# A four-layer graph network on one core: the edge list is written first, and layer 0's scaled rows get four buffers

## The chip, the cores and the metric

The kernel runs on one core of a Trainium2 chip. The core has TensorE (matrix products), VectorE, ScalarE and GpSimd (elementwise work), and SyncE (SP), which issues most DMAs; all run their own instruction streams and meet only at semaphores. The metric is the time of one execution in microseconds (us), lower is better.

## The reference

Four layers work on x, 3125 nodes by 256 features, over one list of 53125 edges (source, destination, weight), sorted by destination. Each adds its result to x and normalises the rows.

```python
x = _layernorm(x + _L0_gnn_ref(x, edge_index, L0_gnn_W, L0_gnn_b), axis=-1)
x = _layernorm(x + _L1_gnn_ref(x, edge_index, edge_weight, L1_gnn_W_rel, L1_gnn_b_rel, L1_gnn_W_root), axis=-1)
x = _layernorm(x + _L2_gnn_ref(x, L2_gnn_W, L2_gnn_att, src, dst), axis=-1)
x = _layernorm(x + _L3_gnn_ref(x, edge_weight, L3_gnn_W, L3_gnn_b, src, dst), axis=-1)
...
# layer 0
h = x @ W
...
deg = jax.ops.segment_sum(ones, col, num_segments=n)
dinv = jnp.where(deg > 0, jax.lax.rsqrt(deg), 0.0)
norm = dinv[row] * dinv[col]
msg = h[row] * norm[:, None]
out = jax.ops.segment_sum(msg, col, num_segments=n)
return jax.nn.relu(out + b)
```

Layers 1 and 3 sum weighted neighbour rows in the same manner; layer 2 is graph attention with 4 heads. The change touches only the preparation and the first loop of layer 0.

## The kernel before

The nodes form NT = 25 tiles of 128 rows (P). Everything is written out by hand, engine by engine, and the order of the code is the order of the work; each engine waits for semaphores with `wait_ge`.

**Preparation.** SP loads the edges as 128 partitions of 416 edges, x, the weights and the biases. VectorE splits each edge into six bf16 fields (LO, CODE, three parts of the weight, panel number) in `tab`; the last field is line 671, after which the semaphore `s_tab` stands at 6. Then it counts degrees: in 26 blocks it writes one-hots of destination digits (lines 690, 691), and TensorE sums them (line 1072). Block b waits for the count of block b-2. After that come attention weights (lines 723 to 733), the span of the destination groups (lines 737 to 756), the degrees (761) and, with ScalarE (479), `dinv` (764).

**What SP sends behind the loads**, in this order: `dst_i`, the destination numbers reordered for layer 2, in pieces of 20 bytes (KC = 5 numbers; lines 317, 319); `src_all`, the source numbers reordered in the same way from DRAM to DRAM (lines 320, 322, 323; the last takes zeros from `spare`); after a wait for `s_tab`, the edge list `flat` (lines 326, 327); after a wait for its landing (`s_flat`), `etab`, 3322 overlapping rows of 128 edges in DRAM (line 330). POOL waits for `etab`, clears an accumulator (441), gathers 32 rows of it (428) and marks which edges belong to the tile (432 to 437); TensorE takes these when it starts the next stage (line 1144). `src_all` is read in layer 1 only (line 357).

**The first loop of layer 0**, over the 25 tiles, makes y = (x W) dinv in three bf16 parts, `y0p[:, t, 0..2]`. TensorE transposes x (line 1119) and multiplies (line 1130). VectorE copies the transposed x out (770). ScalarE's `scaled(t)` writes the f32 row into `u2` (487) and the first part (488). VectorE subtracts, leaving the rest in `u2` (779); ScalarE rounds the rest to the second part (496); VectorE subtracts again for the third part (782, semaphore `b_p3`). `u2` has two buffers, so 487 of tile t waits for 782 of tile t-2. `y0p` lies over the edge table in `big1`, so ScalarE waits for `s_flat` ahead of the loop (line 490). When the last `b_p3` has come, TensorE starts the stage that builds and applies the adjacency matrix, tile by tile; layers 1 to 3 follow.

## Time and profile before

| | us |
|---|---|
| time, median of 3 runs (lowest to highest) | 1800.18 (1798.89 to 1801.12) |
| the profiled execution's own time | 1804.56 |
| its span, first to last instruction | 1802.8 |
| edge list issued by SP | 67.97 |
| first scaled row of the loop (L487) | 81.30 |
| end of the loop (last L782) | 128.70 |

TensorE is busy for 88% of the span, VectorE for 66%. The span is cut into stages with different limits, so these shares say little about one stage. To see what a stage costs, one reads the timeline (start, duration, engine, line, and in brackets the idle time before and what ended it) and looks at which wait ends last. In the span of 1802.8 us, the adjacency stage of layer 0 begins at 129.1 us.

### The profile page before, as it was taken

Reading aid. Unit: us, or ns where it says so; the run is one execution under the profiler, and the core shown is the slowest. Engines: PE = TensorE matmul, PEld = TensorE weight load, DVE = VectorE, ACT = ScalarE, POOL = GpSimd, SP = SyncE. Lnnn points to the kernel's source line nnn. Section 1 sums busy time; section 2 is a strip of 40 time slices with the busy share of each in tenths; the row PEclk is TensorE's granted clock in tenths of the full one; section 3 lists DMA queues with packets and bytes.
Section 4 is the critical chain, followed back from the end, with each engine's and each line's share of the span. In section 5 each row is a group of like instructions: output and inputs, shape, how many; then the busy total and the mean of one; then the engine's idle time right before and its main releaser. Section 6 shows DMA issues by size and latency. Waiting matters only on the chain.

```text
span 1802.8 us, 37754 instructions
## 1 busy us (share of the span) xinstructions
PE 1594.0 (88%) x13731; PEld 1299.1 (72%) x13731; DVE 1186.2 (66%) x2739; ACT 512.2 (28%) x996; POOL 513.5 (28%) x540
## 2 busy tenths in 40 slices
PE   4568999999999899999958888888988877999998
PEld 4448878888888588888835666656666655888887
DVE  8468999999999322222259999998999976112111
ACT  0152232323232000000045555555555544000000
POOL 0022212121211200000157777777777700000000
PEclk9898999999999999999959999998999979999999
DMA  7921212121212434444234444444444421444440
GB/s 136 59 75 77 114 78 113 78 113 78 113 78 112 187 119 159 158 140 144 79 88 112 112 113 113 112 113 112 113 113 113 107 112 37 157 158 161 170 176 17
DMA packets 81220, 203.71 MB, mean 113 GB/s; under 512 B 42635, under 2 KB 57327, under 8 KB 71439
## 3 DMA queue, kind: packets, MB, share of 16 engines
q1 hardware_dynamic: 60047, 141.94, 24.9%
q0 software_dynamic: 20992, 59.37, 12.7%
q8 instruction: 113, 1.85, 0.4%
q14 instruction: 68, 0.56, 0.1%
HBM read 153.00 MB, written 53.57 MB: 115 GB/s over the span
## 4 chain that ended last, share of the span: by engine, by line
PE 55%; POOL 15%; issue 11%; DVE 10%; SPq 4%; DMA 2%; ACT 2%; DVEq 1%; POOLq 0%; ACTq 0%
PE bank L1228 30%; POOL ring L466 15%; PE bank L1172 9%; PE bank L1164 5%; PE bank L1157 2%; PE bank L1190 2%; SPq L322 2%; DVE work L797 2%; PE bank L1314 2%; DMA ring<-attention_rows,work 1%; PE bank L1236 1%; DVE big L810 1%; PE bank L1181 1%; DVE stats L815 1%; DMA edge_list<-big 1%
## 5 line engine op out<-in xcount | busy, mean ns | idle before, releaser
L466 POOL DMA_INDIRECT ring<-attention_rows,work x420 | 399.0, 950 | 149.9 <-issue 146.3
L1228 PE MATMUL bank<-big,ring 128*128 128x256 f32 x1250 | 273.0, 379 | 0.9 <-DVE x_sb L835 0.9
L1228 PE MATMUL bank<-big 128*128 128x256 f32 x1250 | 272.9, 379 | 0.0
L1228 PEld LDWEIGHTS bank<-big,ring 128*128 128x128 f32 x1250 | 236.5, 190 | 33.4 <-DVE x_sb L835 1.7
L1228 PEld LDWEIGHTS bank<-big 128*128 128x128 f32 x1250 | 236.6, 190 | 31.7
L1314 PE MATMUL bank<-work,ring 128*65 128x48 f32 x3360 | 238.6, 232 | 9.7 <-ACT work L587 9.1
L1314 PEld LDWEIGHTS bank<-work,ring 128*65 128x65 f32 x3360 | 227.8, 147 | 18.3 <-ACT work L587 16.2
L1172 PE MATMUL bank<-big 128*128 128x256 bf16 x1875 | 209.0, 273 | 0.9
L1172 PEld LDWEIGHTS bank<-big 128*128 128x128 bf16 x1875 | 181.4, 98 | 25.3 <-ACT big L509 4.7
L587 ACT ACTIVATE work<-work 128x960 f32<-128x960 f32 x84 | 161.8, 1926 | 84.2 <-DVE work L984 83.2
L1053 DVE TENSOR_TENSOR u<-bank,bias 128x256 f32<-128x256 f32 x25 | 10.6, 424 | 211.5 <-PE bank L1228 211.5
L810 DVE SCALAR_TENSOR_TENSOR big<-big,ring,bank 128x400 f32<-128x400 f32 x200 | 125.1, 628 | 35.0 <-PE bank L1164 28.7
L797 DVE TENSOR_TENSOR work<-work,ring 128x1600 bf16<-128x1600 bf16 x156 | 147.4, 985 | 0.0
L1164 PE MATMUL bank<-work 128*128 128x100 bf16 x2400 | 144.9, 209 | 0.0
L514 ACT ACTIVATE std<-mv,epsc 128x1 f32<-128x1 f32 x100 | 29.4, 294 | 386.4 <-DVE mv L816 385.8
L1297 PE MATMUL bank<-ident 128*32 128x512 bf16 x420 | 129.6, 409 | 0.0
L1289 PEld LDWEIGHTS bank<-ident,work 96*128 96x128 f32 x336 | 45.5, 195 | 109.8 <-DVE work L965 107.7
L1164 PEld LDWEIGHTS bank<-work 128*128 128x128 bf16 x2400 | 122.8, 98 | 0.0
L1289 PE MATMUL bank<-ident,work 96*128 96x96 f32 x336 | 59.6, 302 | 67.2 <-DVE work L965 66.5
L428 POOL DMA_INDIRECT ring<-edge_rows,cur x26 | 24.7, 949 | 310.8 <-PE bank L1144 310.7
L509 ACT CAST big<-bank 128x400 bf16<-128x400 f32 x200 | 96.6, 496 | 52.1 <-PE bank L1157 50.6
L951 DVE TENSOR_TENSOR work<-work,bank 128x960 f32<-128x960 f32 x84 | 96.0, 1143 | 0.7 <-issue 0.4
(214 smaller groups left out, 1981.4 us busy)
## 6 DMA issues: line engine op xcount, KB each, us to landing
adjacency<-big SPq DMA_DIRECT2D x25, 1600.0 KB, 5.2
ring<-adjacency SPq DMA_DIRECT2D x25, 1600.0 KB, 7.0
big<-adjacency SPq DMA_DIRECT2D x25, 1600.0 KB, 7.2
ring<-attention_rows,work POOLq DMA_INDIRECT x420
edge_rows<-edge_list SPq DMA_DIRECT2D x1, 4983.0 KB
x_sb<-in_x SPq DMA_DIRECT2D x1, 3072.0 KB
out_x<-xnT SPq DMA_DIRECT2D x24, 128.0 KB, 4.4
work<-attention_rows SPq DMA_DIRECT2D x168, 1.1 KB
```

What stands on the lines that cost most here:

```text
L466: G.indirect_dma_start(out=rows[0:EP, s, c, 0:ZG], out_offset=None, in_=ztab[:, :], in_offset=bass.IndirectOffsetOnAxis(ap=idx[:, g, c:c + ...
L509: S.copy(ac[:, :, q * QUAD * PAN:(q + 1) * QUAD * PAN], cnt_banks[q % 2][:, 0:NT * QUAD * PAN].rearrange("p (b d) -> p b d", b=NT)).then_i ...
L587: S.activation(prob[:, k % 2, :, :], val[:, k % 3].rearrange("p a c -> p c a"), ACT.Exp).then_inc(y["prob_ready"], 1)
L797: ins = V.tensor_tensor(oh[h][2][:, j], oh[h][1], repeated(digs[h][:, W1 + j], NT * PAN), ALU.mult)
L810: V.scalar_tensor_tensor(out=part, in0=part, scalar=keep[:, bass.ds(r, 1)], in1=w_banks[q % 2][:, 0:NT * QUAD * PAN].rearrange("p (b d) -> ...
L951: V.tensor_tensor(val[:, k % 3].rearrange("p (h w) c -> p h w c", h=H), pen[:, k % 3].unsqueeze(1).to_broadcast([EP, H, WIN, KC]), lg.rear ...
L1164: ins = mm(w_banks[b][:, 0:NT * QUAD * PAN].rearrange("p (b d) -> p b d", b=NT)[:, :, cols], lo[:, g, :, m], wtd[:, j, g, :, m].rearrange( ...
L1172: ins = mm(out_banks[t % 2][:, 0:D], ac[:, b, :], y0p[:, b, j, :], start=False, stop=False, skip_group_check=True)
L1228: ins = mm(bank[:, 0:D], slots[s][:, b, :], ybuf[:, b, :], start=(b == 0), stop=(b == NT - 1))
L1289: ins = mm(mb_bank[:, j * 2 * WIN:(j + 1) * 2 * WIN], mg[:, j:j + 1].to_broadcast([2 * WIN, P]), ident[0:2 * WIN, 0:2 * WIN], start=True, ...
L1297: mm(bank[0:32, :].rearrange("p (a b) -> p a b", a=4), ident16[:, 0:32], columns, start=True, stop=True, skip_group_check=True)
L1314: ins = mm(sum_banks[k % 3][0:FH, h * WIN:(h + 1) * WIN], rows[0:EP, s, c, h * FH:(h + 1) * FH], prob[:, k % 2, c, h * WIN:(h + 1) * WIN], ...
```

## The change

The edge list is sent directly behind the bias loads. The destination reordering follows it, then the edge rows `etab`, then the source reordering. `spare` becomes a tile of its own, outside `big1`. The scaled rows go into `ys`, with DEPTH = 4 buffers, carved out of `work`. On VectorE the second subtraction of a tile is made two tiles later, ahead of the first subtraction of the tile in hand.

```diff
+DEPTH = 4
...
+        spare = sb("spare", [EP, KC], I32)
...
-        spare = carve(EP, KC, dt=I32)
...
+        carve = carver(work)
+        ys = carve(P, DEPTH, D)
...
+            sp.wait_ge(s_tab, 6)
+            sp.dma_start(flat[0:P * COLS, :].rearrange("(p e) f -> p e f", p=P), tab[:]).then_inc(s_flat, 16)
+            sp.dma_start(flat[P * COLS:P * COLS + GRAN, :].rearrange("(a e) f -> a e f", a=1),
+                         tab[P - 1:P, COLS - GRAN:COLS, :]).then_inc(s_flat, 16)
             sp.dma_start(dst_i[:, 0:FULL, :], dst[0:FULL * EP * KC].rearrange("(g p k) -> p g k", p=EP, k=KC)).then_inc(
                 ld_dsti, 16)
             sp.dma_start(dst_i[0:REST, FULL, :], dst[FULL * EP * KC:E].rearrange("(p k) -> p k", k=KC)).then_inc(ld_dsti, 16)
+            sp.wait_ge(s_flat, 32)
+            sp.dma_start(etab[:, :], bass.AP(flat.tensor, 0, [[GRAN * FIELDS, ROWS + 1], [1, P * FIELDS]])).then_inc(s_etab, 16)
             sp.dma_start(src_all[:, 0:FULL, :], src[0:FULL * EP * KC].rearrange("(g p k) -> p g k", p=EP, k=KC)).then_inc(
                 s_srcs, 16)
...
-            sp.wait_ge(s_tab, 6)
...
-            sp.wait_ge(s_flat, 32)
...
-                if t >= 2:
-                    act.wait_ge(b_p3, t - 1)
+                if t >= DEPTH:
+                    act.wait_ge(b_p3, t - DEPTH + 1)
                 h = out_banks[t % 2][:, 0:D]
-                S.activation(u2[:, t % 2, :], h, ACT.Copy, scale=dinv[:, t:t + 1]).then_inc(b_y, 1)
+                S.activation(ys[:, t % DEPTH, :], h, ACT.Copy, scale=dinv[:, t:t + 1]).then_inc(b_y, 1)
...
-                    S.copy(y0p[:, t - 1, 1, :], u2[:, (t - 1) % 2, :]).then_inc(b_p2, 1)
+                    S.copy(y0p[:, t - 1, 1, :], ys[:, (t - 1) % DEPTH, :]).then_inc(b_p2, 1)
...
-            for t in range(NT + 1):
+            for t in range(NT + 2):
                 if t + 1 < NT:
                     xT_copy(t + 1)
+                if t >= 2:
+                    v = ys[:, (t - 2) % DEPTH, :]
+                    dve.wait_ge(b_p2, t - 1)
+                    V.tensor_tensor(y0p[:, t - 2, 2, :], v, y0p[:, t - 2, 1, :], ALU.subtract).then_inc(b_p3, 1)
                 if t < NT:
+                    v = ys[:, t % DEPTH, :]
                     dve.wait_ge(b_y, t + 1)
                     dve.wait_ge(b_p1, t + 1)
-                    V.tensor_tensor(u2[:, t % 2, :], u2[:, t % 2, :], y0p[:, t, 0, :], ALU.subtract).then_inc(b_r1, 1)
-                if t >= 1:
-                    dve.wait_ge(b_p2, t)
-                    V.tensor_tensor(y0p[:, t - 1, 2, :], u2[:, (t - 1) % 2, :], y0p[:, t - 1, 1, :],
-                                    ALU.subtract).then_inc(b_p3, 1)
+                    V.tensor_tensor(v, v, y0p[:, t, 0, :], ALU.subtract).then_inc(b_r1, 1)
```

SP's order behind the bias loads, before (tile names without buffer numbers; `big` holds `dst_i` and `tab`, `source_nodes` is `src_all`, `edge_list` is `flat`, `edge_rows` is `etab`):

```order
L316 DMA bias<-in_L_gnn_b 128x256
L317 DMA big<-in_dst 128x83x5
L319 DMA big<-in_dst 1x5
L320 DMA source_nodes<-in_src 128x83x5
L322 DMA source_nodes<-in_src 5x1
L323 DMA source_nodes<-big 127x5
L326 DMA edge_list<-big 128x2496
L327 DMA edge_list<-big 1x96
L330 DMA edge_rows<-edge_list 3322x768
```

and in the changed kernel, whose lines are numbered a little higher:

```order
L320 DMA bias<-in_L_gnn_b 128x256
L322 DMA edge_list<-big 128x2496
L323 DMA edge_list<-big 1x96
L325 DMA big<-in_dst 128x83x5
L327 DMA big<-in_dst 1x5
L329 DMA edge_rows<-edge_list 3322x768
L330 DMA source_nodes<-in_src 128x83x5
L332 DMA source_nodes<-in_src 5x1
L333 DMA source_nodes<-spare 127x5
```

The edge list moved from behind both reorderings to ahead of them, and the edge rows to between them.

VectorE at the start of the loop before, with the buffer numbers (L770 copies transposed x, L779 is the first subtraction, L782 the second):

```order
L770 COPY xnT<-bank1 128x256
L779 TENSOR_TENSOR u<-u,big1 128x256
L782 TENSOR_TENSOR big1<-u,big1 128x256
L770 COPY xnT<-bank6 128x256
L779 TENSOR_TENSOR u<-u,big1 128x256
L782 TENSOR_TENSOR big1<-u,big1 128x256
```

and in the changed kernel (L773 the copy, L787 the first subtraction, L782 the second):

```order
L773 COPY xnT<-bank6 128x256
L782 TENSOR_TENSOR big1<-work,big1 128x256
L787 TENSOR_TENSOR work<-work,big1 128x256
L773 COPY xnT<-bank1 128x256
L782 TENSOR_TENSOR big1<-work,big1 128x256
L787 TENSOR_TENSOR work<-work,big1 128x256
```

The second subtraction stands ahead of the first now and belongs to the tile two before; the scaled rows lie in `work` in place of `u`.

## Rows read from the trace of the kernel before

**Rows 1.** Page, section 4: shares of the span by line, of the chain that ended last.

```profile
PE bank L1228 30%; POOL ring L466 15%; PE bank L1172 9%; PE bank L1164 5%; PE bank L1157 2%; PE bank L1190 2%; SPq L322 2%; DVE work L797 2%; PE bank L1314 2%; DMA ring<-attention_rows,work 1%; PE bank L1236 1%; DVE big L810 1%; PE bank L1181 1%; DVE stats L815 1%; DMA edge_list<-big 1%
```

**Rows 2.** Timeline, SP: start us, us, engine, line, operation, destination<-source, count.

```profile
22.52 0.43 SPq L317 DMA_DIRECT2D big<-in_dst  x1
...
31.21 2.59 SPq L320 DMA_DIRECT2D source_nodes<-in_src  x1
...
33.84 33.62 SPq L322 DMA_DIRECT2D source_nodes<-in_src  x1
...
67.97 1.23 SPq L326 DMA_DIRECT2D edge_list<-big  x1
...
81.30 0.80 SPq L330 DMA_DIRECT2D edge_rows<-edge_list  x1
```

**Rows 3.** Timeline: last field, dinv, first products, first scaled row [idle before <-releaser].

```profile
17.93 0.86 DVE L671 CAST big<-big 128x416 bf16<-128x416 f32 x1
...
69.29 0.32 DVE L764 RECIPROCAL dinv<-dinv 128x25 f32<-128x25 f32 x1 [0.29 <-ACT dinv L479]
...
70.05 2.08 PE L1130 MATMUL bank<-ring,xnT 128*128 128x256 f32 x4
...
72.35 1.92 PE L1130 MATMUL bank<-ring,xnT 128*128 128x256 f32 x4
...
81.30 0.47 ACT L487 ACTIVATE u<-bank,dinv 128x256 f32<-128x256 f32 x1 [12.04 <-DMA edge_list<-big]
```

**Rows 4.** Timeline, layer 0's loop, tile 6 (L487 to the next L487).

```profile
92.75 0.47 ACT L487 ACTIVATE u<-bank,dinv 128x256 f32<-128x256 f32 x1 [0.69 <-DVE big L782]
...
93.03 1.13 PE L1130 MATMUL bank<-ring,xnT 128*128 128x256 f32 x4 [0.47 <-DVE xnT L770]
...
93.12 0.47 ACT L488 ACTIVATE big<-bank,dinv 128x256 bf16<-128x256 f32 x1
...
93.48 0.40 ACT L496 CAST big<-u 128x256 bf16<-128x256 f32 x1
...
93.69 0.42 DVE L779 TENSOR_TENSOR u<-u,big 128x256 f32<-128x256 f32 x1 [0.72 <-ACT big L488]
...
94.04 0.42 DVE L782 TENSOR_TENSOR big<-u,big 128x256 bf16<-128x256 f32 x1
...
94.37 0.42 DVE L770 COPY xnT<-bank 128x256 f32<-128x256 f32 x1
...
94.57 0.47 ACT L487 ACTIVATE u<-bank,dinv 128x256 f32<-128x256 f32 x1 [0.69 <-DVE big L782]
```

**Rows 5.** Timeline row of TensorE's restart; windows: busy by engine, PEclk, DMA share, GB/s.

```profile
83.06 2.07 PE L1130 MATMUL bank<-ring,xnT 128*128 128x256 f32 x4 [8.41 <-DVE xnT L770]
...
72.00:76.00 4.00, 2.64 (x9) 1.82 (x7) 0.00 (x0) 0.00 (x0) 0.00 (x0) 1.00 0.91 53
...
84.00:88.00 4.00, 4.00 (x13) 3.09 (x12) 1.17 (x4) 1.83 (x5) 0.00 (x0) 0.50 0.73 276
...
88.00:92.00 4.00, 3.19 (x16) 2.36 (x15) 2.32 (x7) 2.63 (x8) 0.00 (x0) 0.99 0.73 276
```

**Rows 6.** Timeline: last scaled row, and TensorE's first operation of the next stage.

```profile
126.43 0.47 ACT L487 ACTIVATE u<-bank,dinv 128x256 f32<-128x256 f32 x1 [0.68 <-DVE big L782]
...
129.14 0.38 PE L1144 MATMUL bank<-ident,ring 32*128 32x32 bf16 x5 [3.12 <-DVE big L782]
```

**Rows 7.** Timeline and windows: VectorE idle in the counting; stretch 57 to 69 us.

```profile
44.10 0.69 DVE L690 TENSOR_TENSOR work<-ring,big 128x1024 bf16<-128x1024 bf16 x1 [1.78 <-PE bank L1072]
...
55.47 0.69 DVE L690 TENSOR_TENSOR work<-ring,big 128x1024 bf16<-128x1024 bf16 x1 [3.04 <-remote]
...
57.00:69.00 12.00, 4.36 (x28) 3.08 (x26) 9.60 (x32) 0.00 (x0) 0.00 (x0) 1.00 1.51 6
```

**Rows 8.** Timeline: VectorE's first read of dst_i, POOL's first work on etab.

```profile
61.88 0.37 DVE L737 CAST dstf<-big 128x415 f32<-128x415 int32 x1
...
103.77 2.77 POOL L441 MEMSET big<- 128x3200 f32 x1 [100.78 <-DMA edge_rows<-edge_list]
```

More of the change, by code:

```diff
@@ L323, in _ @@
             sp.dma_start(src_all[REST:EP, FULL, :], spare[REST:EP, :]).then_inc(s_srcs, 16)
-            sp.wait_ge(s_tab, 6)
-            sp.dma_start(flat[0:P * COLS, :].rearrange("(p e) f -> p e f", p=P), tab[:]).then_inc(s_flat, 16)
-            sp.dma_start(flat[P * COLS:P * COLS + GRAN, :].rearrange("(a e) f -> a e f", a=1),
-                         tab[P - 1:P, COLS - GRAN:COLS, :]).then_inc(s_flat, 16)
-            sp.wait_ge(s_flat, 32)
-            sp.dma_start(etab[:, :], bass.AP(flat.tensor, 0, [[GRAN * FIELDS, ROWS + 1], [1, P * FIELDS]])).then_inc(s_etab, 16)
             sp.wait_ge(s_nswb, 1)
@@ L629, in _ @@
             V.memset(src_e[96:P, :], 0)
-            V.memset(spare, 0)
+            V.memset(spare[:], 0)
             V.memset(w_e[96:P, :], 0.0).then_inc(s_pad, 1)
```

## The prediction

> **What bounds the kernel now.** I read the page first, then the chain of work that ended last, then the DMA queue's rows, then the timeline of 17 to 130 us. The chain's shares put TensorE and the attention gathers in front, and neither is touched. But the chain also holds 2% on the SP queue's line 322 and 1% on the landing of the edge list [rows 1]. Those are the stretch that the change is about, so only 17 to 129 us has to be worked out; behind it every stage waits for the one before and should just shift.
>
> The reader is to see three things there. First, SP. It issues the 20-byte reordering of the destinations at 22.52 and of the sources at 31.21, and then stands in the issue of the next small transfer, line 322, for 33.62 us, until 67.5. Only then can it issue the edge list (67.97), whose end it waits for before it issues the edge rows at 81.30 [rows 2]. The edge list's last field had been written on VectorE by 18.8 [rows 3]. Second, ScalarE. 1/sqrt(degree) is ready at 69.6 and the product of tile 0 ends at 72.13, yet the first scaled row is written at 81.30, after 12.04 us idle put down to the edge list's landing [rows 3]; it waits for that because y0p lies over the edge table. Third, the loop over 25 tiles that follows is bound by no engine. ScalarE writes the scaled row (L487), writes its bf16 part (L488), VectorE subtracts (L779) and then makes the third part of the tile before (L782), and L782 frees one of two buffers for the next L487. Starts: 92.75, 93.12, 93.69, 94.04, 94.57, that is 0.37 + 0.57 + 0.35 + 0.53 = 1.82 us a tile, while each engine is busy 1.1 to 1.4 of it [rows 4].
>
> **The change part by part.**
>
> *The edge list goes first.* In SP's order its two transfers now stand behind the bias loads, whose last issue ends at 22.5, right ahead of the destinations. The wait for the table (18.8) is over by then, so it adds nothing; queued behind it are the destinations, wanted by VectorE's L737, which starts at 61.88 without idle time [rows 8]. Two issues (1.23 and 0.28 us) push them back by 1.6 of some 30 us to spare. The transfer is 624 KB; alone in the queue I estimate under 6 us, worked out from the edge rows, 4983 KB in at most 22.5 us (81.30 to POOL's start at 103.77) [rows 2, 8]. So it lands before 35. ScalarE's wait then ends with the product of tile 0: 70.05 + 2.08 + about 0.04 = 72.17 in place of 81.30, which is **9.1 us**.
>
> *The wait for the list's landing on SP* now stands behind the destinations. Queued behind it are the edge rows and the three source transfers. SP comes to it after the small destination transfer, near 33, so the edge rows go out then, and land by 33 + 22.5 = 56, where they landed at 103.8. POOL's first memset, gather and three operations took 103.77 to about 111.6 and would be done by 66, then beside VectorE's serial chain; 0 to 0.5 us for that. TensorE wants their result at the end of the loop, so this path stays hidden with some 45 us to spare. The sources come last: issued near 34, moving behind the edge rows, some 57 to 97. Their user is the index load in layer 1, far behind; SP's first adjacency store wants the queue at about 133, and is free by 92.
>
> *spare* moves to a tile of its own: same memset, no cost.
>
> *Four buffers and the later subtraction.* No instruction is added. What binds next? In the new order the subtraction of tile t stands right ahead of the copy of x of tile t+2. So the ring goes copy to product, product to ScalarE, L487 to L779, L779 to copy, and closes after two tiles: 0.48 (94.37 less one period is 92.55, to 93.03) + 1.13 + 0.04 + 0.94 (92.75 to 93.69) + 0.35 = 2.94, **1.47 us a tile** [rows 4]. ScalarE's three alone need 3 x 0.37 = 1.10, VectorE's three 1.03, TensorE about 1.3 to 1.4. Below it the bound is TensorE's 1.3; above it the old 1.82. I take 1.47, as every link of it is a row. The buffers themselves are behind by then: L487 of tile t waits for the third part of tile t-4, which stands two tiles back on VectorE.
>
> *How the loop runs.* L487 of tile 0 at 72.17; tile 1 at 72.35 + 1.92 + 0.04 = 74.31 [rows 3]; the product of tile 2 can start at 74.5. Its pace is the question. In 83 to 88 four passes took 2.07 us at a granted clock of 0.50, the lower level (1.2 GHz), after idle time; from 88 on the row says 0.99, the upper level (2.4 GHz), and they take 1.13 [rows 4, 5]. At 70 to 74 they also take 2.08, though the row there says 1.00 [rows 5]: I go by the durations, as low. The restart at 83.06 took about 4.9 us of work; from the first transpose at 68.9 that gives 73.8. So tile 2 runs fast: L487 at 75.7. Each tile that stays slow costs 2.14 less 1.47, so 0 to 4 tiles more are 0 to 2.7 us; I take 0 and keep the end.
> The Trainium skill (TensorE: Matmul & The Clock Gate, "Seeing it yourself") warns that clock events in a trace have been unreliable. By that the column at 72 to 76 is wrong and the sum stands; by the column the slowness of the first two products would have another cause, and if that lasted over the loop, 22 tiles at 2.14 would add 15 us, which the fast tiles from 88 on speak against.
>
> Tile 24: 75.7 + 22 x 1.47 = 108.0. From L487 of tile 6 (92.75) to tile 24 (126.43) before, 18 periods took 33.68, 0.9 more than 18 x 1.82; I keep that 0.9. The tail, last L487 to the end of the last L782, is 128.70 - 126.43 = 2.27, and TensorE starts the next stage on it [rows 6]. End: 108.0 + 0.9 + 2.3 = 111.2 against 128.70, **17.5 us** in all: 9.1 from the wait, 8.4 from the loop.
>
> *What is not in the rows.* While the sources moved, VectorE stood idle four times in 42 to 56 us, 1.78, 0.47, 0.88 and 3.04 us (6.2 in all), with the counts that it waits for already made by the order of the work; the first and last stand in [rows 7]. None stands in its 18 blocks before, and none in 57 to 69, when the sources were still moving (DMA share 1.51, 6 GB/s) [rows 7]. If the reordering causes them, they leave this stretch, which is serial before the loop, -6.2 us. They may then come back in 72 to 97: 6.2 in the 27 us from 42 to 69 is 0.23 a us, times 25 us, +5.7. If it does not, 0. All three middles are near zero, so I take 0 and keep -6.2 and +5.7 for the range.
>
> **The rivals.**
> *The stalls leave and do not come back*: the loop asks for fewer instructions a us than the counting did, and 57 to 69 had none. 1782.7 - 6.2 = 1776.5.
> *The loop hardly quickens*: another ring, a slow clock or returning stalls keep it at 1.7 to 1.82. For it: three engines hand on to each other five times a tile, and each hand-over is only known from the old order. Against it: no link of the old ring is left. With 1.82, 22 x 0.35 = 7.7 comes back: 1790.4; with 1.65, 1786.7.
> *It does not do what it says*: the edge list lands no earlier than the degrees, or the edge rows (POOL) become the late ones. It would need them 45 us later than worked out. Within 3 us of 1800.
> *Slower*: one mechanism, the source reordering beside the loop. A stall of the mean kind seen (6.2/4 = 1.55 us) on VectorE has nothing to hide it, since the four buffers cover ScalarE and not VectorE's own queue. Place: L782 and L787 of the changed loop, 72 us to its end. It decides from 17.5/1.55 = 11.3, so 12 stalls in 25 tiles undo the gain, and one in every tile gives 25 x 1.55 = 38.8 less 17.5, +21: 1821. Against it: four stalls in 27 us of the same transfers, and none in the last 12.
>
> **How the numbers follow.** The profiled execution took 1804.56 us, its span 1802.8 and 1.8 around it; the median of the runs shown is 1800.18, 4.4 lower, and I take the same difference off both: 1787.1 for a profiled execution, 1800.18 - 17.5 = **1782.7** as the time. Chances: forecast within 3.5 us 0.46; stalls leave or a period nearer 1.3, 0.18; slow loop 0.27; no effect 0.05; slower 0.04. The range 1774 to 1792 takes the first three with their ends (1776.5 less up to 2.5 for a shorter period; 1790.4 and 1.6 for the clock), and leaves 0.14. Faster by over 0.2% (3.6 us, about what a measurement can tell from no change) 0.93, within it 0.03, slower 0.04.
>
> **What would show it.** SP: the edge list issued near 23, no wait of ScalarE for it, its first L490 near 72.2. Edge rows issued near 33 and POOL's first memset before 60. In the loop L490 to L490 alternating about 1.2 and 1.7, mean 1.47; TensorE's first turn of fields near 111.5. The adjacency, attention and last layers as long as before. Wrong would be: POOL later than TensorE at the loop's end, a mean period over 1.65, "remote" or unexplained idle time on VectorE between 72 and 97, or VectorE waiting for the destinations at L740.

## The result and the profile after

The changed kernel takes 1778.49 us (median of 4 runs, 1777.58 to 1779.33) against 1799.54 us of the kernel before (4 runs, 1797.31 to 1801.12): a ratio of 0.9885, 95% interval 0.9869 to 0.9901, that is 21.05 us less. 1782.7 with a range of 1774 to 1792 was forecast. The profiled execution took 1778.9 us, its span 1777.1; the profiled one before lies 5.0 above the median of its four runs, so the two traces differ by more than the times do, 25.7 us.

Of these 25.7 us, 25.15 lie ahead of the first operation of the adjacency stage, which TensorE starts at 103.99 instead of 129.14. The rows in the order of the steps, first SP's (timeline; columns as in [rows 2]):

```profile
20.47 0.43 SPq L322 DMA_DIRECT2D edge_list<-big  x1
20.95 0.29 SPq L323 DMA_DIRECT2D edge_list<-big  x1
21.28 0.38 SPq L325 DMA_DIRECT2D big<-in_dst  x1
21.70 8.56 SPq L327 DMA_DIRECT2D big<-in_dst  x1
30.31 2.46 SPq L329 DMA_DIRECT2D edge_rows<-edge_list  x1
32.81 13.18 SPq L330 DMA_DIRECT2D source_nodes<-in_src  x1
46.03 43.77 SPq L332 DMA_DIRECT2D source_nodes<-in_src  x1
```

The edge list leaves at 20.47 instead of 67.97 [rows 2], the edge rows at 30.31 instead of 81.30. The long issue has not gone: SP stands 43.77 us in L332, but nothing that is wanted soon is queued behind it. Its next job, the first adjacency store, is at 125.82.

The serial part and the first tile (timeline, the changed kernel; L767 is L764 of before, L1134 is L1130, L490 is L487, L782 and L787 are the second and the first subtraction, L1148 is L1144):

```profile
62.67 0.32 DVE L767 RECIPROCAL dinv<-dinv 128x25 f32<-128x25 f32 x1 [0.29 <-ACT dinv L482]
63.43 2.08 PE L1134 MATMUL bank<-ring,xnT 128*128 128x256 f32 x4
65.60 0.47 ACT L490 ACTIVATE work<-bank,dinv 128x256 f32<-128x256 f32 x1 [2.96 <-PE bank L1134]
65.72 1.19 PE L1134 MATMUL bank<-ring,xnT 128*128 128x256 f32 x4
...
103.99 0.38 PE L1148 MATMUL bank<-ident,ring 32*128 32x32 bf16 x5 [2.74 <-DVE big L782]
```

Against [rows 3] two things are seen. ScalarE's wait for the edge list (12.04 us) is now a wait for the product, 2.96 us. And `dinv` itself is there at 62.67 instead of 69.29, 6.6 us earlier, which the change does not touch directly. The loop (two tiles; compare [rows 4], where one took 1.82 us):

```profile
89.34 0.47 ACT L490 ACTIVATE work<-bank,dinv 128x256 f32<-128x256 f32 x1 [0.70 <-PE bank L1134]
...
90.28 0.43 DVE L787 TENSOR_TENSOR work<-work,big 128x256 f32<-128x256 f32 x1 [0.74 <-ACT big L491]
90.43 0.47 ACT L490 ACTIVATE work<-bank,dinv 128x256 f32<-128x256 f32 x1
90.62 0.42 DVE L773 COPY xnT<-bank 128x256 f32<-128x256 f32 x1
...
91.10 1.13 PE L1134 MATMUL bank<-ring,xnT 128*128 128x256 f32 x4 [0.49 <-DVE xnT L773]
...
92.27 0.47 ACT L490 ACTIVATE work<-bank,dinv 128x256 f32<-128x256 f32 x1 [0.71 <-PE bank L1134]
```

Two tiles take 2.93 us, 1.09 and 1.84 in turn. ScalarE's idle time now ends on the product and no longer on the second subtraction. From tile 2 (68.52) to tile 24 (101.28) the mean is 1.489.

POOL's path (timeline; compare 103.77 in [rows 8]):

```profile
72.45 2.77 POOL L444 MEMSET big<- 128x3200 f32 x1 [69.46 <-DMA edge_rows<-edge_list]
75.38 1.22 POOL L431 DMA_INDIRECT ring<-edge_rows,cur  x1 [0.17 <-issue]
94.50 0.32 POOL L435 TENSOR_SCALAR cur<-cur 32x1 int32<-32x1 int32 x1 [17.90 <-DMA ring<-edge_rows,cur]
94.91 1.06 POOL L437 TENSOR_SCALAR ring<-ring,panel 32x128 bf16<-32x128 int16 x1
96.05 0.61 POOL L440 TENSOR_TENSOR ring<-ring 32x128 bf16<-32x128 bf16 x1
```

It is done at 96.7, 7.3 us ahead of TensorE's first turn of the next stage; some 45 us were forecast.

The chain that ended last, by engine, in shares of the span, before and after:

```profile
PE 55%; POOL 15%; issue 11%; DVE 10%; SPq 4%; DMA 2%; ACT 2%; DVEq 1%; POOLq 0%; ACTq 0%
PE 57%; POOL 15%; DVE 13%; issue 12%; ACT 1%; DMA 1%; DVEq 1%; POOLq 0%; SPq 0%; ACTq 0%
```

SP's 4% are gone, and the DMA's 2% are 1%; that 1% is the attention rows' landing. The large lines of [rows 1] keep their shares.

### The profile page after: what moved, and what is told of

Same layout as the page of the kernel before. It is cut to its first block, busy times and chain, and to the rows that moved or that the text cites. A ratio compares the mean times of both kernels' runs of the same rounds, so it can differ in the third digit from the quotient of the medians.

```text
span 1777.1 us, 37754 instructions
## 1 busy us (share of the span) xinstructions
PE 1588.4 (89%) x13731; PEld 1296.0 (73%) x13731; DVE 1186.3 (67%) x2739; ACT 511.2 (29%) x996; POOL 514.9 (29%) x540
## 3 DMA queue, kind: packets, MB, share of 16 engines
q8 instruction: 113, 1.85, 0.4%
## 4 chain that ended last, share of the span: by engine, by line
PE 57%; POOL 15%; DVE 13%; issue 12%; ACT 1%; DMA 1%; DVEq 1%; POOLq 0%; SPq 0%; ACTq 0%
PE bank L1232 30%; POOL ring L469 15%; PE bank L1176 9%; PE bank L1168 5%; PE bank L1161 2%; PE bank L1194 2%; DVE work L801 2%; PE bank L1318 1%; PE bank L1240 1%; DVE big L814 1%; DMA ring<-attention_rows,work 1%; PE bank L1134 1%; ACT work L590 1%; PE bank L1185 1%; DVE stats L819 1%
```

## The experiments

The kernels again to two_buffers ran on one chip (the kernel before there: 1802.99 us, 9 runs), src_mid to sub_late on another (1803.55, 7 runs), and the last four on a third, on which everything, the kernel before too (1969.48, 9 runs), ran at a lower granted clock: mean 0.88 to 0.89 over the span there, 0.95 to 0.97 elsewhere. Each ratio is to the kernel before on the same chip. The changed kernel was not run again in these groups, so where a kernel is set against it, ratios or places in the traces are compared, not times. "Us a tile" is the period where nothing disturbs it and, in brackets, the mean from tile 2 to tile 24, both from L490 (L487 before). "Next stage" is TensorE's first operation of the adjacency stage in the trace.

| kernel | time, us | ratio to before (95%) | dinv | first scaled row | us a tile | next stage |
|---|---|---|---|---|---|---|
| before, [rows 3, 6] | 1799.54 | | 69.29 | 81.30 | 1.82 (1.88) | 129.14 |
| changed | 1778.49 | 0.9885 (0.9869 to 0.9901) | 62.67 | 65.60 | 1.465 (1.49) | 103.99 |
| again (before, one run) | 1801.33 | | 66.38 | 80.05 | 1.82 (1.85) | 127.31 |
| order_only | 1788.49 | 0.9918 (0.9905 to 0.9932) | 62.73 | 65.65 | 1.82 (1.86) | 113.06 |
| loop_only | 1795.39 | 0.9959 (0.9945 to 0.9972) | 69.84 | 80.32 | 1.46 (1.50) | 119.78 |
| two_buffers | 1795.07 | 0.9954 (0.9939 to 0.9970) | 62.46 | 65.38 | 2.15 (2.16) | 119.38 |
| src_mid | 1783.68 | 0.9895 (0.9878 to 0.9911) | 65.20 | 68.12 | 1.46 (1.48) | 107.32 |
| src_last | 1787.72 | 0.9910 (0.9893 to 0.9926) | 62.65 | 65.58 | 1.82 (1.86) | 113.07 |
| src_late | 1784.24 | 0.9895 (0.9878 to 0.9911) | 65.87 | 68.80 | 1.46 (1.48) | 107.37 |
| sub_late | 1774.52 | 0.9837 (0.9821 to 0.9854) | 62.65 | 65.57 | 1.085 (1.26) | 99.19 |
| src_late_gate | 1945.65, lower clock | 0.9871 (0.9855 to 0.9888) | 62.61 | 65.54 | 1.46 (1.49) | 104.02 |
| direct_gate | 1943.30, lower clock | 0.9862 (0.9847 to 0.9877) | 62.71 | 65.63 | 1.46 (1.49) | 103.97 |
| direct_sub_late | 1940.95, lower clock | 0.9847 (0.9830 to 0.9863) | 66.54 | 69.47 | 1.085 (1.08) | 99.55 |
| best | 1936.95, lower clock | 0.9823 (0.9810 to 0.9836) | 63.07 | 65.99 | 1.085 (1.08) | 95.60 |

### Do VectorE's idle pieces come back, and does their size hold?

**again** is the kernel before, unchanged.

> The kernel before, word for word, for a second profile. What it tells apart is the 6.2 us that VectorE stood idle in four pieces between 42 and 56 us of the first profile. Theory A (the source reordering in flight causes them, in every execution): at least two idle pieces, 3 to 9 us in all, while the degree counts run, and the loop's first scaled row at 80 to 82 us. Theory B (they were chance in that one profiled execution): less than 1 us idle there, the counts done by about 50, the first scaled row still held by the edge list, and the profiled time nearer to the median (1797 to 1801) than to 1804.6. In both: 1.82 us a tile in the loop.

Measured: 1801.33 us. VectorE's idle time in the counting (timeline):

```profile
44.77 0.69 DVE L690 TENSOR_TENSOR work<-ring,big 128x1024 bf16<-128x1024 bf16 x1 [2.81 <-remote]
...
49.88 0.69 DVE L690 TENSOR_TENSOR work<-ring,big 128x1024 bf16<-128x1024 bf16 x1 [0.52 <-PE bank L1072]
...
51.47 0.69 DVE L690 TENSOR_TENSOR work<-ring,big 128x1024 bf16<-128x1024 bf16 x1 [0.42 <-PE bank L1072]
```

With `dinv` at 66.38, and

```profile
80.05 0.47 ACT L487 ACTIVATE u<-bank,dinv 128x256 f32<-128x256 f32 x1 [13.70 <-DMA edge_list<-big]
```

The pieces of idle time recur, at other places and of another size: 3.75 us here, 6.2 in the first trace. They delay `dinv` and nothing else: the first scaled row waits for the edge list's landing either way, so in the kernel before they are hidden behind that wait.

### The two halves of the change

**order_only** has SP's new order and the loop of before:

```diff
+            sp.wait_ge(s_tab, 6)
+            sp.dma_start(flat[0:P * COLS, :].rearrange("(p e) f -> p e f", p=P), tab[:]).then_inc(s_flat, 16)
...
             sp.dma_start(dst_i[:, 0:FULL, :], dst[0:FULL * EP * KC].rearrange("(g p k) -> p g k", p=EP, k=KC)).then_inc(
                 ld_dsti, 16)
...
+            sp.wait_ge(s_flat, 32)
+            sp.dma_start(etab[:, :], bass.AP(flat.tensor, 0, [[GRAN * FIELDS, ROWS + 1], [1, P * FIELDS]])).then_inc(s_etab, 16)
             sp.dma_start(src_all[:, 0:FULL, :], src[0:FULL * EP * KC].rearrange("(g p k) -> p g k", p=EP, k=KC)).then_inc(
                 s_srcs, 16)
...
-            sp.wait_ge(s_tab, 6)
-            sp.dma_start(flat[0:P * COLS, :].rearrange("(p e) f -> p e f", p=P), tab[:]).then_inc(s_flat, 16)
...
-            sp.wait_ge(s_flat, 32)
-            sp.dma_start(etab[:, :], bass.AP(flat.tensor, 0, [[GRAN * FIELDS, ROWS + 1], [1, P * FIELDS]])).then_inc(s_etab, 16)
```

> The changed order of SP's transfers and spare as a tile of its own, with the loop of the kernel before (two buffers, old place of the second subtraction). My sum: the wait goes, 9.1 us, and the loop stays at 1.82 us a tile, so 1799.5 - 9.1 = 1790.4, ratio 0.9949. Theory A adds the stalls that leave the counting: 9 + 3 to 6, so 1784 to 1787, ratio 0.992 to 0.993, first scaled row at 65 to 67 us and no idle time of VectorE in the counting. Theory B: 1789 to 1791 in time. Rival: the sources now move beside the loop, and if they hold VectorE up there, the loop takes over 1.95 us a tile and the gain is under 5 us.

Measured: 14.5 us faster. VectorE has no idle time in the counting, `dinv` is at 62.73, and the loop keeps 1.82.

**loop_only** has the four buffers and the later subtraction, with SP's order of before (it leaves out what the diff above shows).

> Four buffers and the second subtraction two tiles later, with SP's order of the kernel before. The two-tile ring gives 1.47 us a tile: first scaled row still at about 81 us, last one near 118, gain 8.4 us, 1791.1, ratio 0.9953. The rival, that the loop quickens only because it starts while TensorE is still warm or because nothing else moves, gives under 5 us here. The idle pieces in the counting stay as in the kernel before (theory A: 3 to 9 us; theory B: none).

Measured: 7.6 us faster. The idle pieces are there again (2.42, 1.10 and 2.27 us in the counting and 0.72 at 61.22, right behind it, 6.5 in all), `dinv` at 69.84, and ScalarE waits for the list again:

```profile
80.32 0.47 ACT L491 ACTIVATE work<-bank,dinv 128x256 f32<-128x256 f32 x1 [10.51 <-DMA edge_list<-big]
```

So the two halves hardly share anything: 14.5 + 7.6 = 22.1 against 21.05 together, within what such medians can tell. The loop gives about what was forecast for it (8.4). The order gives more than its 9.1.

### The ring in the loop

**two_buffers** is the changed kernel with half the buffers:

```diff
-DEPTH = 4
+DEPTH = 2
```

> The changed kernel with DEPTH = 2: the second subtraction stays two tiles later, but the scaled rows have two buffers again. Following the links of the trace: the scaled row of tile t now waits for a subtraction that itself stands behind the copy of x of tile t+1, which gives about 2.1 us a tile in place of 1.46, 16 us more over the loop: about 1794, ratio to the kernel before 0.997. If the buffers did nothing and the place of the subtraction alone made the gain, it would stay at 1778.5 (0.9885).

Measured (timeline, ScalarE):

```profile
88.79 0.47 ACT L490 ACTIVATE work<-bank,dinv 128x256 f32<-128x256 f32 x1 [1.38 <-DVE big L782]
...
90.94 0.47 ACT L490 ACTIVATE work<-bank,dinv 128x256 f32<-128x256 f32 x1 [1.02 <-DVE big L782]
...
93.08 0.47 ACT L490 ACTIVATE work<-bank,dinv 128x256 f32<-128x256 f32 x1 [1.02 <-DVE big L782]
```

2.15 us a tile: L490 of tile t waits for the third part of tile t-2, which now stands behind the copy of the next x. The later subtraction alone makes the loop slower than before; only with the buffers is it a gain. The loop is 15.6 us longer than in the changed kernel in the traces, as expected; the ratio (0.9954 against the expected 0.997) says some 12 us. Four buffers with the subtraction at its old place were not run. By the links of [rows 4] their ring would be that of 2.94 us and one subtraction more (94.04 to 94.37), (2.94 + 0.33) / 2 = 1.64 us a tile, an estimate: half of the gain.

**sub_late** goes one step on. The ring of two tiles (copy, product, scaled row, first subtraction, copy) is opened by making the first subtraction one tile later too, with six buffers:

```diff
-DEPTH = 4
+DEPTH = 6
...
-            for t in range(NT + 2):
+            for t in range(NT + 3):
                 if t + 1 < NT:
                     xT_copy(t + 1)
-                if t >= 2:
-                    v = ys[:, (t - 2) % DEPTH, :]
-                    dve.wait_ge(b_p2, t - 1)
+                if 3 <= t:
+                    v = ys[:, (t - 3) % DEPTH, :]
+                    dve.wait_ge(b_p2, t - 2)
...
-                if t < NT:
-                    v = ys[:, t % DEPTH, :]
+                if 1 <= t <= NT:
+                    v = ys[:, (t - 1) % DEPTH, :]
...
```

> A shorter ring: the changed kernel with the first subtraction of a tile one tile later, the second three tiles later, and six buffers. Then the copy of x no longer stands behind the subtraction of the tile before, and by the trace's links TensorE binds at 1.17 us a tile in place of 1.46: last scaled row near 94 and end of the loop at 96.3, 7 us earlier. But POOL's gather, slow beside the sources, gives its result at 96.7 to 98 (94.5 to 98.0 in three traces for its first step after landing, plus 2.2), so that path would bind, and TensorE starts the next stage at 97 to 101: gain over the changed kernel 3 to 6.5 us, ratio 0.985 to 0.987. Rival: the ring was not what bound the loop, and it stays at 1.46 with a ratio of 0.9885.

Measured: 1774.52 us, 29.0 under before, ratio 0.9837 where 0.985 to 0.987 was expected. The ring was the bound, but what binds next is not TensorE at 1.17 us a tile: the rows of ScalarE are now back to back, 3 x 0.36 us, 1.085 us a tile:

```profile
80.77 0.47 ACT L490 ACTIVATE work<-bank,dinv 128x256 f32<-128x256 f32 x1
81.15 0.47 ACT L491 ACTIVATE big<-bank,dinv 128x256 bf16<-128x256 f32 x1
81.50 0.40 ACT L499 CAST big<-work 128x256 bf16<-128x256 f32 x1
81.86 0.47 ACT L490 ACTIVATE work<-bank,dinv 128x256 f32<-128x256 f32 x1
```

POOL's result, expected to be the late one, is there at 97.6; the next stage (99.19) ends its wait on the second subtraction. The profiled execution also lost time to a stall of TensorE in 89 to 91 us, while the sources were still moving:

```profile
91.19 0.38 PE L1134 MATMUL bank<-ring,xnT 128*128 128x256 f32 x1 [1.99 <-issue]
...
91.62 1.91 PE L1134 MATMUL bank<-ring,xnT 128*128 128x256 f32 x4
```

After 2.0 us in which TensorE waited for nothing that the profile shows, the next products take 1.91 us in place of 1.03; the granted clock of 92 to 94 us is 0.50, the lower level. Three periods of 3.24, 1.96 and 1.89 us come of it, 3.8 us over 3 x 1.085. The changed kernel's trace has no such gap in its loop.

### Which transfer makes VectorE idle, and what sources cost elsewhere

**src_mid** is the changed kernel with the source transfers (all three) put ahead of the edge rows again, so that only the edge list goes early:

```diff
             sp.dma_start(dst_i[:, 0:FULL, :], dst[0:FULL * EP * KC].rearrange("(g p k) -> p g k", p=EP, k=KC)).then_inc(
                 ld_dsti, 16)
...
+            sp.dma_start(src_all[:, 0:FULL, :], src[0:FULL * EP * KC].rearrange("(g p k) -> p g k", p=EP, k=KC)).then_inc(
+                s_srcs, 16)
...
             sp.wait_ge(s_flat, 32)
             sp.dma_start(etab[:, :], bass.AP(flat.tensor, 0, [[GRAN * FIELDS, ROWS + 1], [1, P * FIELDS]])).then_inc(s_etab, 16)
-            sp.dma_start(src_all[:, 0:FULL, :], src[0:FULL * EP * KC].rearrange("(g p k) -> p g k", p=EP, k=KC)).then_inc(
-                s_srcs, 16)
...
```

> The changed kernel with the source reordering ahead of the edge rows in place of behind them: edge list, destinations, sources, edge rows. The sources then move from 34 to about 72 us, beside the degree counts, as in the kernel before, while ScalarE's wait for the edge list stays gone. Theory A (sources moving beside the counts make VectorE stand idle there): 3 to 6 us of idle pieces between 42 and 57, the loop's start at 69 to 72, and 3 to 6 us more than the changed kernel, ratio to before 0.990 to 0.992. Theory C (the pieces came from SP's long stand in one issue or from the late edge list, not from this traffic): none, ratio 0.9885. The edge rows land near 95 and POOL ends near 100, under the loop's end at 104 to 110.

Measured: VectorE's idle pieces are back, 1.07, 0.27, 0.69, 0.15 and 0.27 us (2.45 in all, under the 3 to 6 expected), and now they count: `dinv` is at 65.20 and the first scaled row at 68.12, 2.5 later than in the changed kernel. The ratio, 0.9895 (0.9878 to 0.9911), is too near 0.9885 to tell the two theories apart; the trace does. At the loop's end POOL's path is the late one, which was not expected:

```profile
99.58 2.77 POOL L444 MEMSET big<- 128x3200 f32 x1 [96.59 <-DMA edge_rows<-edge_list]
...
107.32 0.38 PE L1148 MATMUL bank<-ident,ring 32*128 32x32 bf16 x5 [3.79 <-POOL ring L440]
```

**src_last** is order_only with the edge list behind the destinations in place of ahead of them:

```diff
-            sp.wait_ge(s_tab, 6)
-            sp.dma_start(flat[0:P * COLS, :].rearrange("(p e) f -> p e f", p=P), tab[:]).then_inc(s_flat, 16)
...
             sp.dma_start(dst_i[:, 0:FULL, :], dst[0:FULL * EP * KC].rearrange("(g p k) -> p g k", p=EP, k=KC)).then_inc(
                 ld_dsti, 16)
...
+            sp.wait_ge(s_tab, 6)
+            sp.dma_start(flat[0:P * COLS, :].rearrange("(p e) f -> p e f", p=P), tab[:]).then_inc(s_flat, 16)
...
             sp.wait_ge(s_flat, 32)
             sp.dma_start(etab[:, :], bass.AP(flat.tensor, 0, [[GRAN * FIELDS, ROWS + 1], [1, P * FIELDS]])).then_inc(s_etab, 16)
```

> The loop of the kernel before (two buffers), and SP's order destinations, edge list, edge rows, sources: only the source reordering is moved behind, the edge list stays behind the destinations. If the sources alone held the edge list and VectorE, this is worth as much as the whole new order, ratio 0.9918 as there, with the edge list issued near 31 and landed before 45. If the place ahead of the destinations matters as well, it gives back more than 2 us. The chain asks for the list at 65 us only, so I expect no difference.

Measured: the same as order_only, next stage at 113.07 against 113.06, with the list issued at 30.17. SP issues the edge rows at 36.70, so the list has landed by then. The gain of the order is all in what passes the sources; the place ahead of the destinations adds nothing.

**src_late** holds the sources back until POOL's first gather has landed:

```diff
             sp.wait_ge(s_flat, 32)
             sp.dma_start(etab[:, :], bass.AP(flat.tensor, 0, [[GRAN * FIELDS, ROWS + 1], [1, P * FIELDS]])).then_inc(s_etab, 16)
+            sp.wait_ge(c_gath, 16)
             sp.dma_start(src_all[:, 0:FULL, :], src[0:FULL * EP * KC].rearrange("(g p k) -> p g k", p=EP, k=KC)).then_inc(
                 s_srcs, 16)
...
```

> The changed kernel with one wait more on SP: the source reordering is issued when POOL's first gather of edge rows has landed. The first gather took 17.9 us beside the sources and 1.9 us in the kernel before; and the edge rows, issued near 31, landed by 72 where I had worked out 56. Without the sources beside them: edge rows landed by 54 to 58, gather 2 us, POOL's result before 66 in place of 96.7. TensorE asks for it at 104, so the time should not move: ratio 0.988 to 0.989. If the sources slow the loop of 25 tiles, it would change by over 2 us as they move 30 us later and meet its end.

Measured: POOL's memset starts at 54.19 instead of 72.45 and the gather's wait is 1.83 us instead of 17.90, as in the kernel before (1.92). But the kernel is not faster: the first scaled row comes 3.2 us later than in the changed kernel. Two operations of VectorE in the serial part are stretched (timeline, VectorE; the second block shows the same operations in the changed kernel):

```profile
55.24 1.94 DVE L741 CAST dstf<-big 128x415 f32<-128x415 int32 x1
62.65 1.84 DVE L756 TENSOR_SCALAR wide<-steps,span 128x66 f32<-128x66 f32 x1
```

```profile
55.26 0.37 DVE L740 CAST dstf<-big 128x415 f32<-128x415 int32 x1
61.03 0.26 DVE L755 TENSOR_SCALAR wide<-steps,span 128x66 f32<-128x66 f32 x1
```

1.57 + 1.58 = 3.15 us, the whole delay. Beside them POOL runs its two memsets, 54.19 to 56.96 and 61.55 to 64.43, and each stretched operation ends within 0.25 us of the end of its memset, 57.18 and 64.49. The theory from this run: the memset holds these operations up. The sources cannot be the cause of the first, since SP issues them at 59.69 only. By the Trainium skill (SBUF — State Buffer, "Who interferes with whom") a VectorE cast or tensor_scalar in its two-port mode and a GpSimd instruction exclude one another for a whole instruction, while a VectorE instruction with two SBUF inputs meets only a GpSimd instruction that reads SBUF, not one that only writes it. The two rows agree, though no trace tells the mode. So does the loop of the changed kernel: beside the memset at 72.45, copies out of PSUM and subtractions keep their 0.42 us, and beside POOL's TENSOR_TENSOR at 96.05, which reads SBUF, one subtraction takes 0.67.

**src_late_gate** tests that. It is src_late with POOL's first memset held until `dinv` is written, that is, past the serial part:

```diff
             pool.wait_ge(s_etab, 16)
+            pool.wait_ge(s_dinv, 1)
```

> src_late with one wait more: POOL starts its work on the edge rows only when 1/sqrt(degree) is ready. In src_late the two memsets of POOL (2.77 and 2.88 us) fell beside VectorE's serial chain, where a cast took 1.94 us in place of 0.37 and an operation on 128x66 took 1.84 in place of 0.26, 3.2 us in all, the same 3.2 us by which the loop began late (68.80 for 65.60). If the memsets are the cause, the loop begins at 65.6 again and the ratio goes from 0.9895 to 0.988. If the later source traffic is the cause, the loop still begins 3 us late or takes over 2 us longer.

Measured: the delay is gone, and the cast takes 0.37 us again and the operation on 128x66 0.26.

```profile
63.26 2.77 POOL L446 MEMSET big<- 128x3200 f32 x1 [60.27 <-DVE dinv L769]
...
65.54 0.47 ACT L492 ACTIVATE work<-bank,dinv 128x256 f32<-128x256 f32 x1 [2.96 <-PE bank L1136]
```

First scaled row 65.54, next stage 104.02, the changed kernel's places to within 0.1 us. The gate also puts the sources' issue later, at 68.68; they still move beside the loop. The ratios, 0.9871 and src_late's 0.9895, have intervals that overlap, so the proof is in the traces. A cleared source queue gives nothing by itself, as long as TensorE waits for VectorE and not for POOL.

**direct_gate** takes the slow kind of transfer away. The sources go in 20-byte pieces into SBUF and from there in long rows to DRAM, again with POOL held:

```diff
-            sp.dma_start(src_all[:, 0:FULL, :], src[0:FULL * EP * KC].rearrange("(g p k) -> p g k", p=EP, k=KC)).then_inc(
-                s_srcs, 16)
...
+            sp.dma_start(src_i[:, 0:FULL, :], src[0:FULL * EP * KC].rearrange("(g p k) -> p g k", p=EP, k=KC)).then_inc(
+                s_src_in, 16)
+            sp.dma_start(src_i[0:REST, FULL, :], src[FULL * EP * KC:E].rearrange("(p k) -> p k", k=KC)).then_inc(s_src_in, 16)
+            sp.wait_ge(s_src_in, 32)
+            sp.dma_start(src_all, src_i).then_inc(s_srcs, 16)
...
             pool.wait_ge(s_etab, 16)
+            pool.wait_ge(s_dinv, 1)
```

> The changed kernel, with the sources reordered into SBUF (20-byte pieces, as the destinations are) and from there to DRAM in long rows, and with POOL's work held until 1/sqrt(degree) is ready. The destinations took about 10 us into SBUF where the sources took some 40 from DRAM to DRAM. If it is the target of the pieces that makes them slow, the sources land within 15 us of their issue, SP is free before 65 in place of 90, and POOL's first gather takes 2 us in place of 17.9. The time should stay at the changed kernel's, ratio 0.988 to 0.989, as none of this is waited for.

Measured: SP stands 9.93 us in the second source transfer instead of 43.77, and the rows go out to DRAM at 58.67 where the last piece was issued at 89.84. The sources are in SBUF 25 us after their first issue (33.54), where 15 were expected; the edge rows move ahead of them. The gather's wait is 1.77. The next stage starts at 103.97, as in the changed kernel: some 30 us less of traffic beside the loop, and no difference in the loop.

**direct_sub_late** has the same sources and the loop of sub_late, and no gate for POOL.

> The shorter ring of sub_late with the sources by way of SBUF, without the wait on POOL. The loop at 1.09 us a tile, no late instruction block of TensorE (2.0 us idle at 89 in sub_late) and no wait for POOL. But the edge rows land near 54, so both memsets fall beside VectorE's serial chain again: the loop begins 1.5 to 3.2 us late. Next stage on TensorE at 97.5 to 99.5; ratio about 0.985.

Measured: the memset at 54.82 meets the cast again, and the second one the operation on 128x66 (1.85 us); the first scaled row is at 69.47 in place of 65.6, 3.9 us late where 1.5 to 3.2 was expected:

```profile
55.06 2.75 DVE L741 CAST dstf<-big 128x415 f32<-128x415 int32 x1
```

The loop then runs at 1.085 without a gap on TensorE, next stage 99.55. That the gap in sub_late was a late instruction block, as the expectation calls it, no run shows.

**best** puts the three together: sources by way of SBUF, the loop of sub_late, POOL held for `dinv`.

> The same with POOL held until 1/sqrt(degree) is ready: shorter ring, sources by way of SBUF, memsets out of the serial chain. Loop from 65.6, 1.09 us a tile, last scaled row near 93, next stage on TensorE at 95.5 to 97 in place of 104.0 in the changed kernel: 8 us less, ratio 0.982 to 0.984. If another wait takes the place (POOL's memset beside the loop's subtractions, or the clock), it stays over 0.9845.

Measured, as expected: ratio 0.9823 (0.9810 to 0.9836), the lowest of all, though sub_late's interval on its own chip overlaps it; 32.5 us under before in its group. Its loop has no gap, and the next stage starts 8.4 us earlier than in the changed kernel:

```profile
95.60 0.38 PE L1150 MATMUL bank<-ident,ring 32*128 32x32 bf16 x5 [2.75 <-DVE big L784]
```

Against direct_gate, in the same group, the ratio is 1936.95/1943.30 = 0.9967, 6.4 us.

## Why the prediction was right, and where it was not

**The wait for the edge list: right.** The list was forecast to leave near 23 and left at 20.47; ScalarE no longer waits for it. The first scaled row was to come at 72.17 and came at 65.60. The 15.7 us in the traces are the 9.1 of this term and the 6.6 by which `dinv` is earlier. order_only shows that the order alone does this (65.65, 14.5 us in the time).

**The idle pieces: the mis-sized term.** They were taken at zero net, with -6.2 and +5.7 kept as ends. They left and did not come back, the rival with 0.18. What the runs add is which transfer goes with them. The four traces with the sources moving beside the counting have them (before 6.2 us [rows 7], again 3.75, loop_only 6.5, src_mid 2.45); of the ten traces with the edge rows there instead, none has. src_mid against the changed kernel leaves little else: the edge list is early in both, and the pieces come with the sources. With the sources comes SP's long stand in their issue; no run parts the two, but in the changed kernel SP stands there from 32.81 on (L330, L332) and the counting, which ends at 50.0, has no piece. The windows show what moves while the counting ends, before and after (columns as in [rows 5]; the last three are PEclk, DMA share and GB/s):

```profile
48.00:52.00 4.00, 3.17 (x49) 2.79 (x48) 3.07 (x7) 0.00 (x0) 0.00 (x0) 1.00 1.23 6
52.00:56.00 4.00, 1.05 (x16) 0.93 (x16) 0.96 (x2) 0.00 (x0) 0.00 (x0) 1.00 1.67 6
```

```profile
40.00:44.00 4.00, 3.40 (x57) 3.04 (x54) 3.91 (x9) 0.00 (x0) 0.00 (x0) 1.00 0.73 276
44.00:48.00 4.00, 3.56 (x56) 3.07 (x55) 3.89 (x8) 0.00 (x0) 0.00 (x0) 1.00 0.75 280
48.00:52.00 4.00, 3.78 (x53) 3.48 (x52) 3.81 (x10) 0.00 (x0) 0.00 (x0) 1.00 1.42 140
```

Before, 20-byte pieces move at 6 GB/s and VectorE is busy 0.96 of 4 us in one slice. A full queue is not needed: the first piece of idle time falls into 40 to 44 us, where the DMA share is 0.28. After, the edge rows run at 276 to 280 GB/s until 48, with the sources queued behind them, and VectorE is busy 3.8 to 3.9 of 4.

The weak step is how three cases became one number. The prediction had -6.2 if the pieces leave, -0.5 if they come back in the loop, and 0 if they have nothing to do with the transfer; it called all three near zero and took 0, though the first is not near zero and none is a loss.

The size needs care too. In the kernel before the pieces do not move the loop's start, since again and loop_only reach the first scaled row at 80.05 and 80.32, with 3.75 and 6.5 us of pieces. Larger pieces only leave less of the wait. A path hidden behind a wait should have been priced twice: as it is, and without the traffic that the change takes away from beside it. Measured by again, the pieces are 3.7 us and the wait is 10.7 us, 14.4 in all, which is what order_only gives in the time (14.5); the first trace has 6.6 and 9.1, 15.7 in all.

With the loop's 8.4 the order's 14.4 make 22.8 us, against 21.05 measured, whose interval goes from 17.8 to 23.6. The forecast's 17.5 and the rival's 23.7 lie just outside it on either side. So the forecast is short by the term that it took at zero, and 1.8 us between 22.8 and 21.05 stay unaccounted for.

**The loop: right.** Forecast was 1.47 us a tile by the ring of two tiles; measured are 1.465 undisturbed and 1.489 as the mean of 22 tiles, where 1.47 with the 0.9 us of disturbances would make 1.51. Opening that ring (sub_late, which needs six buffers for it) gave 1.085, and closing the other one (two_buffers) 2.15. The tail was 2.71 us from the last L490 to TensorE, as in [rows 6]. The alternation came out stronger than expected (1.09 and 1.84 late in the loop, 1.36 and 1.56 at its start). The rival of a loop at 1.65 to 1.82 fell.

**The clock: 0 taken, and 0.6 us gained.** The first product takes 2.08 us, as long as at a granted clock of 0.50 [rows 5], and the second 1.19 already; two slow ones were expected, so tile 2 starts 2.92 us after tile 0, not 3.5. The clock's own column says 1.00 for all of 62 to 67 us, so the durations alone speak for the clock.

The steps add up: 17.5 + 6.6 (`dinv`) + 0.6 (tile 2 earlier) + 0.5 (a shorter loop from there, 32.76 us for 33.24) = 25.2, and the traces differ by 25.15 at the next stage.

**POOL's path: wrong by a long way, and lucky.** The edge rows were to land at 56, and POOL starts on them at 72.45; the 20-byte sources issued 2.5 us behind them share the queue (DMA share 1.42 in 48 to 52, against 0.73 with the edge rows alone). The gather was priced at its old 1.92 us and waited 17.90. Both are undone in src_late (54.19 and 1.83). Of "45 us to spare" 7.3 are left. src_mid shows the next limit: with the edge rows behind the sources, this path ends last. The luck is in the other term: POOL's work beside VectorE's serial chain was priced at 0 to 0.5 us, and src_late, where the rows land as early as forecast, pays 3.15 for it. The changed kernel is spared this only because they land late.

**The slower rival, stalls of VectorE in the loop,** did not occur: the loop of the changed kernel has no idle piece of this kind, with the sources moving until about 91. One stall did occur in a loop, of TensorE, in sub_late.

**The destinations** at L740 were read at 55.26 without a wait, as expected.

**What stays open** is by what path small DRAM to DRAM pieces stop VectorE or TensorE. The traces call the idle time "remote" or put it down to counts that had long been made. No instruction packet is recorded within the stalls of before, again and loop_only. In sub_late one lies right ahead of the gap on TensorE (DMA by queue, 88.0 to 89.2 us). The changed kernel's loop has such packets too, one in 85 to 90 us and one in 90 to 91.5, and no gap, so this is no more than a coincidence so far:

```profile
q14 instruction: 1, 0.01, 17.4%
```

Nor is it known why the counting meets the idle pieces and the loop hardly does.

## What to carry to other kernels

Before pricing a transfer that is moved, list what stands behind it in its queue and which serial work lies beside it, at the old place and at the new one; a path that is hidden today becomes the bound with the delays that today's wait hides. In a loop in which no engine is full, write down the rings (chains of waits that come back to their start) with their length and the number of tiles after which each closes, and change the one with the largest quotient. Here the later step alone made it worse (two_buffers: 2.15 us a tile), four buffers with the later step gave 1.465, and one more step later, with six buffers, 1.085, ScalarE's own time. Work on GpSimd that becomes possible earlier is not free if VectorE is on the critical path then.

## What the runs showed of the hardware that was not expected

- A memset of 128x3200 f32 on GpSimd (2.77 and 2.88 us) stretched a VectorE cast from 0.37 to 1.94 us and a tensor_scalar from 0.26 to 1.84 (src_late; 2.75 and 1.85 in direct_sub_late), and left f32 copies out of PSUM and tensor_tensor alone (changed kernel, 72.45 to 75.2). Holding the memset back took the delay away (src_late_gate, best).
- Beside GpSimd's operations on 32x128, some VectorE subtractions of two SBUF tiles took 0.58 to 0.70 us in place of 0.42 (changed 96.13, before 111.08, order_only 98.75, direct_gate 69.49 and 70.36, best 70.00 and 70.87); others there kept 0.42 (src_late_gate, sub_late).
- The reordering of 53125 numbers in 20-byte pieces from DRAM to DRAM keeps SP in its second issue for 30 to 44 us (30.49 in src_late_gate, 44.48 in src_last); the same pieces into SBUF for 9.93 us (direct_gate).
- Beside these pieces a gather of 32 rows waits 17.9 to 22.8 us (changed, order_only, src_last, two_buffers, sub_late), and 1.7 to 2.0 without them. The Trainium skill (DMA: Bandwidth & Descriptors, "Queues, rings and completion order") says that a DMA engine serves its queues in turn, packet by packet; the trace agrees, and gives the price: in the changed kernel 11 packets of POOL's queue move in 75 to 85 us beside 2190 of SP's, and 18 in the next 5 us, beside 858.
- While the counting ran beside the same pieces, VectorE lost 2.45 to 6.5 us in three to five stalls (before, again, loop_only with one right behind the counting, src_mid), another amount in each execution. The cause is open.
